# Attention stage: the values of two groups in one visit, and the first-pass products put elsewhere in the written-out order

## The chip, the cores and the metric

The kernel runs on one core of a Trainium2 chip. The metric is the device time of one execution in microseconds. A core has TensorE (PE: matrix products; its weight loads are listed apart as PEld), VectorE (DVE), ScalarE (ACT), GpSimd (POOL) and SyncE (SP, which here issues transfers). Each engine works through its own instructions in order, and the engines wait for each other through semaphores. TensorE writes its products to PSUM, which has eight banks; VectorE and ScalarE read them from there.

## The reference, cut to what matters

Two transformer layers follow each other. The change touches only the attention of the first one: two sequences of 2048 rows, 256 channels, 16 heads of 16 channels, a causal mask.

```python
Q = relu(x @ Wq + bq); K = relu(x @ Wk + bk); V = relu(x @ Wv + bv)   # (2, 2048, 256), 16 heads
scores = einsum('bqhd,bkhd->bhqk', Qh, Kh) / sqrt(16)
scores = where(key_mask == 0, NEG, scores); scores = where(tril == 0, NEG, scores)
attn = softmax(scores, axis=-1) * query_mask
out = einsum('bhqk,bkhd->bqhd', attn, Vh)        # then out + x, a normalisation, gamma and beta
```

What comes before it (normalisation, projections, a first pair of expert products) and after it (a second attention with landmarks, an expert layer) is the same in both kernels.

## The kernel before

The function `attention` works in 8 rounds of 4 heads (`n` from 0 to 7; a round is 4 of the 16 heads of one of the two sequences). The softmax needs the largest score of each query row before the exponentials can be taken, so the scores are computed twice, in two layouts.

**First pass** (`first`, 80 steps in a round, 640 in all). One step multiplies one tile of 128 queries with up to 512 keys for two heads at once, each head on 64 rows of TensorE (L993, two products side by side, into one of two slots of `c_pf`). VectorE then takes the largest score of each row: of a full stretch for both heads in one `TENSOR_REDUCE` (L1159, 48 in a round), and of the stretch with the diagonal, 128 to 512 keys wide, head by head with the mask added (L1155, 32 steps in a round). A slot is free again when VectorE is through with it (`free_slot`: a wait on `c_max_ok` for the last but one user). After the last step of a block of 512 queries six small VectorE steps (`max`) make the row maxima ready in three bf16 parts, TensorE turns them (`rows`, L999, also a user of a slot), VectorE copies them (L1182), and SP writes them with four transfers as three further rows of `c_qa`, so that the score product subtracts them itself.

**Second pass** (`score`, 36 groups of 4 steps in a round, one step per head). A group is a tile of 128 keys against a block of 512 queries, on the diagonal two smaller pieces; its steps use the full 128 rows and columns (L1012, on the diagonal also L1016 for the mask) and go into one of three slots of `c_pst`. ScalarE takes the exponential of each (L1051) into `c_prob`, which holds three groups. **Values** (`values`, one step per group): the four heads side by side, each on 32 columns of TensorE, in float32, which takes two passes (8 products, L1028), summed up in the one bank `c_po`. After the last group of a block of queries VectorE copies the bank out (`take`, L1187), TensorE turns it (`turn`, L1037, also a user of a slot of `c_pf`) and VectorE divides by the sums (L1195 to L1202).

**The order** of all these steps is one list, `steps`, made by `plan()`; every engine walks the same list and takes out its own. In the kernel before, `plan()` adds first-pass steps ahead of each score step for as long as their share of the whole lies less than `lead` ahead of the scores' share; `first_steps` does that, and puts two of the pending `max` steps behind each. The values of group j - 2 follow the fourth score of group j (`LAG`). So TensorE goes `score, first, score, score, first, score, values` in most groups. First-pass steps run about half a round ahead of the scores that need them, and the last 75 scores have none beside them; there VectorE works on the sum with the residual (`ahead`, L1066 to L1102), one piece at a time.

## Time and profile before

| | us |
|---|---|
| median of 3 runs | 2183.31 (2177.08 to 2183.34) |
| profiled execution, first to last instruction | 2184.2 |
| attention, first product to last turn | 297.0 to 1252 |
| TensorE busy over the span | 1842.2 (84%) |
| VectorE busy over the span | 1511.6 (69%) |
| ScalarE busy over the span | 1045.4 (48%) |

The profile is one execution. Times in its rows are microseconds from the start of the span; a row of a timeline has the start, the duration, the engine, the line, the operation with what it writes and reads, the count, and in brackets how long the engine had been idle before it and what ended that. Products are pipelined: a product of 512 columns shows 0.39 us, but the next one starts after less. So TensorE's pace is read from the distance between two starts, not from durations, and its busy time says little about how much room it has. The same goes to a smaller degree for VectorE, whose next instruction starts just ahead of the end of the one before.

### The profile page before, as it was taken

To read this page: it belongs to the slowest core of one execution; us is meant where nothing else is said; L and a number is where in the kernel's file an instruction comes from. 1 tells how busy PE (TensorE), PEld (TensorE's weight loads), DVE (VectorE), ACT (ScalarE), POOL (GpSimd) and SP (SyncE) were. 2 spreads that over 40 slices of the span, in tenths; PEclk is the share of its full clock that TensorE was granted. 3 is DMA by queue.
4 is the path that set the end of the run, shared out by engine and by line. 5 is a ranking of instruction groups with operands and counts; after the bars stand their busy time and mean duration, and the time that the engine had idled before them with its cause. 6 is when DMAs were issued, how large, how long until landed. Compare 5 with 4: busy or idle time off the path is not lost. (4 is left out here: it accounts for less than half of the span.)

```text
span 2184.2 us, 36363 instructions
## 1 busy us (share of the span) xinstructions
PE 1842.2 (84%) x13023; PEld 968.6 (44%) x13023; DVE 1511.6 (69%) x3492; ACT 1045.4 (48%) x1949; POOL 536.0 (25%) x592
## 2 busy tenths in 40 slices
PE   0998926899999999999899869799339788999998
PEld 0565602222222222222223246565239565888865
DVE  7986656888888888888788854387115797344456
ACT  3554403466666676666666735365003354323210
POOL 1443350000000000000330000100740786566620
PEclk9999958999999999999999979899559799999999
DMA  3466563013030304040620163000410622566656
GB/s 97 140 219 213 188 155 66 1 31 120 18 133 12 139 3 148 2 149 2 226 79 11 47 241 126 1 1 3 170 70 4 216 93 95 173 186 188 186 200 221
DMA packets 158721, 238.82 MB, mean 109 GB/s; under 512 B 19762, under 2 KB 127282, under 8 KB 156882
## 3 DMA queue, kind: packets, MB, share of 16 engines
q1 hardware_dynamic: 122706, 152.46, 23.0%
q0 software_dynamic: 23136, 75.65, 9.4%
q10 hardware_dynamic: 12704, 8.39, 1.2%
q8 instruction: 108, 1.77, 0.3%
q14 instruction: 67, 0.55, 0.1%
HBM read 116.23 MB, written 119.82 MB: 108 GB/s over the span
## 5 line engine op out<-in xcount | busy, mean ns | idle before, releaser
L1051 ACT ACTIVATE c_prob<-c_pst 128x512 f32<-128x512 f32 (+1 forms) x1152 | 602.9, 573 | 359.5 <-PE c_pst L1012 218.3
L1159 DVE TENSOR_REDUCE c_mx<-c_pf 128x2 f32<-128x1024 f32 x384 | 462.9, 1222 | 90.3 <-PE c_pf L993 87.4
L1012 PE MATMUL c_pst<-c_qa,c_ka 128*128 128x512 bf16 (+3 forms) x1280 | 394.0, 358 | 37.2 <-DMA c_qa<-c_mT 33.6
L993 PE MATMUL c_pf<-c_ka,c_qa 64*128 64x512 bf16 (+3 forms) x1280 | 234.5, 363 | 77.1 <-DVE c_mx L1159 26.4
L1028 PE MATMUL c_po<-c_prob,c_vh 128*32 128x512 f32 (+3 forms) x2560 | 297.2, 547 | 1.5 <-DVE c_osb L1187 0.5
L1155 DVE CUSTOM_DVE_ANT_0 c_spare<-c_pf,c_cut 128x384 f32<-128x384 f32 (+3 forms) x512 | 231.1, 491 | 51.9 <-PE c_pf L993 47.3
L1012 PEld LDWEIGHTS c_pst<-c_qa,c_ka 128*128 128x128 bf16 x1280 | 108.7, 97 | 283.1 <-ACT c_prob L1051 122.2
L993 PEld LDWEIGHTS c_pf<-c_ka,c_qa 64*128 64x128 bf16 x1280 | 61.9, 93 | 310.9 <-issue 126.4
L925 POOL IOTA c_zero<- 128x24 int32 x6 | 1.3, 215 | 696.8 <-PE c_po L1028 696.8
L1980 POOL DMA_INDIRECT s_parts<-x_yr,x_tags x144 | 141.0, 979 | 84.9 <-DVE x_yr L2604 61.6
L2488 PE MATMUL x_ps<-x_gu,x_xs 128*128 x576 | 136.8, 380 | 0.0
L1980 POOL DMA_INDIRECT s_slots<-x_rows,place x128 | 125.7, 982 | 37.5 <-issue 30.7
L2589 DVE TENSOR_TENSOR x_h<-x_ps,x_sg 128x256 f32<-128x256 f32 x72 | 30.6, 424 | 141.5 <-ACT x_sg L2558 134.0
L2488 PEld LDWEIGHTS x_ps<-x_gu,x_xs 128*128 128x128 f32 x576 | 104.4, 191 | 11.3
L1016 PE MATMUL c_pst<-c_negk,c_idb 128*128 128x128 bf16 x512 | 95.9, 221 | 0.0
L1028 PEld LDWEIGHTS c_po<-c_prob,c_vh 128*32 128x32 f32 x2560 | 54.6, 109 | 86.4 <-issue 42.3
L2145 DVE SCALAR_TENSOR_TENSOR i_X<-i_pm,i_eyes 128x256 f32<-128x256 f32 x48 | 20.1, 424 | 101.0 <-PE i_pm L2078 97.1
L2551 ACT COPY x_xs<-x_ps 128x512 f32<-128x512 f32 x72 | 42.2, 586 | 84.4 <-issue 65.9
L2509 PE MATMUL x_ps<-x_d,x_hT 128*128 x288 | 74.1, 380 | 0.0
L365 POOL TENSOR_TENSOR b_parts<-b_r,b_parts 128x512 bf16<-128x512 f32 x32 | 56.9, 1796 | 57.8 <-ACT b_parts L502 57.8
L1411 PE MATMUL e_pq<-e_xs,e_w 128*128 128x512 f32 x128 | 61.1, 629 | 9.5 <-ACT QT L1353 9.5
L2558 ACT ACTIVATE x_sg<-x_ps 128x256 f32<-128x256 f32 x72 | 27.7, 384 | 82.8 <-PE x_ps L2488 74.8
(378 smaller groups left out, 3007.1 us busy)
## 6 DMA issues: line engine op xcount, KB each, us to landing
s_slots<-c_zero POOLq DMA_DIRECT2D x6, 3264.0 KB, 20.4
x_xr<-s_slots SPq DMA_DIRECT2D x72, 272.0 KB
x_rows<-s_parts SPq DMA_DIRECT2D x8, 2048.0 KB, 8.7
c_qa<-s_qs SPq DMA_DIRECT2D x64, 192.0 KB, 9.0
c_ka<-s_ks SPq DMA_DIRECT2D x64, 192.0 KB, 9.8
s_qs<-b_parts SPq DMA_DIRECT2D x32, 256.0 KB, 2.4
s_ks<-b_parts SPq DMA_DIRECT2D x32, 256.0 KB, 2.7
s_vs<-b_va SPq DMA_DIRECT2D x32, 256.0 KB, 3.7
```

Of the source, the lines that this page charges most:

```text
L365: nc.gpsimd.tensor_tensor(parts[:, i, 2, :], r[:, i, :], parts[:, i, 1, :], ALU.subtract).then_inc(parts_ok, 1)
L993: mm = nc.tensor.matmul(pf[:, slot, h - fh, 0:kn], qa[r, s, h, qt * P:(qt + 1) * P], ka[r, s, h, k0:k0 + kn], start=True, stop=True, tile_ ...
L1012: mm = nc.tensor.matmul(pst[:, u % NS, at:at + qn], ka[:, s, hh, kt * P:(kt + 1) * P], qa[:, s, hh, qb * QB + q0:qb * QB + q0 + qn], start ...
L1016: mm = nc.tensor.matmul(pst[:, u % NS, at:at + P], idb[:], negk[:], start=False, stop=True)
L1028: mm = nc.tensor.matmul(po[HV * h:HV * h + HV, q0:q0 + qn], vh[:, s, kt, h, :], prob[:, a % NP, h, at:at + qn], start=(kt == 0), stop=(a i ...
L1051: nc.scalar.activation(prob[:, g % NP, hh, 0:w], pst[:, u % NS, 0:w], ACT.Exp).then_inc(exp_ok, 1)
L1155: ins = nc.vector.tensor_tensor_reduce(spare[:, h, 0:kn], pf[:, slot, h, 0:kn], cut[:, W1 - kn:], 1.0, 0.0, ALU.add, ALU.max, mx[:, fh + h ...
L1159: nc.vector.tensor_reduce(mx[:, fh:fh + 2, qt, part], pf[:, slot, :, 0:kn], AX.X, ALU.max).then_inc(max_ok, 1)
L1411: mm = nc.tensor.matmul(pq[:, i % 2, :], w[:, k, i * P:(i + 1) * P], xs[:, s, k, :], start=(k == 0), stop=(k == K - 1))
L1980: return nc.gpsimd.indirect_dma_start(out=dst, out_offset=bass.IndirectOffsetOnAxis(ap=index.bitcast(U32), axis=0), in_=src, in_offset=None)
L2488: mm = nc.tensor.matmul(pgu[:, m % 2, i, :], xs[:, m % 2, i, k, :], gu[:, k, bass.ds(e, 1), :].rearrange("p o n -> p (o n)"), start=(k == ...
L2509: mm = nc.tensor.matmul(pyr[:, m % 2, i, :], hT[:, m % 2, i, :], d[:, bass.ds(e, 1), :].rearrange("p o n -> p (o n)"), start=True, stop=True)
```

## The change

Everything lies in `plan()`; no engine's code and no buffer is touched.

- Within a block of 512 queries the groups are taken two by two. The values of both are multiplied in one visit, behind the scores of the group after them; since a block has 3, 7, 11 or 15 groups, its last one has a visit of its own. A round has 16 visits of two groups and 4 of one, in the place of 36.
- First-pass steps are put in at fewer points: ahead of a visit, behind it, and between two visits of pairs behind the third and the sixth of the eight scores (where a visit of one group follows, behind the second of its four).
- `lead` starts at 0.3 in the place of 0.21 and is capped at 0.56 in the place of 0.52. Ahead of the first score the first-pass steps are given out in 15 portions, with the `rows` step of the first block among them.
- A turn comes two groups behind the last group of its block in the place of three groups behind.

```diff
-    LAG, NP = 2, 3
+    NP = 3
     assert NG % NP == 0
+    visits = []
+    for qb in range(NB):
+        of = [g for g in range(NG) if groups[g][0] == qb]
+        visits += [of[i:i + 2] for i in range(0, len(of), 2)]
+    visit_of = {n * NG + v[-1]: [n * NG + g for g in v] for n in range(NQ) for v in visits}
+    breaks = {}
+    for n in range(NQ):
+        for v in visits:
+            for g in v:
+                breaks[n * NG + g + 1] = (3, 6) if len(v) == 2 else (2,)
+    breaks[0] = (2,)
...
     def lead(s):
-        return min(0.52, 0.21 + 0.6 * s)
+        return min(0.56, 0.3 + 0.6 * s)
...
-        for j in range(NQ * NG + LAG + 1):
+        def point(now, due=None):
+
+            first_steps(passed + lead(passed) if due is None else due)
+            if waiting and (len(steps) >= waiting[0][0] + 6 or now >= NQ * NG):
+                _, m, qb = waiting.pop(0)
+                steps.append(("rows", m, qb, 0))
+
+        for i in range(1, 16):
+            point(0, lead(0) * i / 15)
+        since = 0
+        for j in range(NQ * NG + 2):
             n, g = divmod(j, NG)
             for hh in range(HQ):
                 if n < NQ:
-                    first_steps(passed + lead(passed))
-                if waiting and (len(steps) >= waiting[0][0] + 6 or n == NQ):
-                    _, m, qb = waiting.pop(0)
-                    steps.append(("rows", m, qb, 0))
-                if done == NQ * N1:
-                    chain_step()
-                if n < NQ:
+                    if done == NQ * N1:
+                        chain_step()
                     steps.append(("score", n, g, hh))
                     passed += width[g] / sum(width) / HQ
-            if LAG <= j < NQ * NG + LAG:
-                vn, vg = divmod(j - LAG, NG)
-                steps.append(("values", vn, vg, 0))
...
+                since += 1
+                if since in breaks.get(j, ()):
+                    point(j)
+            if j - 1 in visit_of:
+                point(j)
+                for i in visit_of[j - 1]:
+                    vn, vg = divmod(i, NG)
+                    steps.append(("values", vn, vg, 0))
+                    if vg in last:
+                        steps.append(("take", vn, last.index(vg), 0))
+                point(j)
+                since = 0
+            if j >= 2 and (j - 2) % NG in last:
+                tn, tg = divmod(j - 2, NG)
+                steps.append(("turn", tn, last.index(tg), 0))
```

TensorE in the middle of the fourth round (`n` = 3), from the scores of group 13 to the values of groups 12 and 13, before. `c_pst` is written by scores, `c_pf` by first-pass steps and `c_po` by values:

```order
L1028 MATMUL c_po<-c_prob,c_vh 32x512 x4
L1012 MATMUL c_pst<-c_qa,c_ka 128x512
L993 MATMUL c_pf<-c_ka,c_qa 128x512 x2
L1012 MATMUL c_pst<-c_qa,c_ka 128x512 x2
L993 MATMUL c_pf<-c_ka,c_qa 128x512 x2
L1012 MATMUL c_pst<-c_qa,c_ka 128x512
L1028 MATMUL c_po<-c_prob,c_vh 32x512 x4
L1012 MATMUL c_pst<-c_qa,c_ka 128x512
L993 MATMUL c_pf<-c_ka,c_qa 128x512 x2
L1012 MATMUL c_pst<-c_qa,c_ka 128x512 x2
L993 MATMUL c_pf<-c_ka,c_qa 128x512 x2
L1012 MATMUL c_pst<-c_qa,c_ka 128x512
```

The same engine and place in the changed kernel:

```order
L1050 MATMUL c_po<-c_prob,c_vh 32x512 x8
L1034 MATMUL c_pst<-c_qa,c_ka 128x512 x3
L1015 MATMUL c_pf<-c_ka,c_qa 128x512 x4
L1034 MATMUL c_pst<-c_qa,c_ka 128x512 x3
L1015 MATMUL c_pf<-c_ka,c_qa 128x512 x2
L1034 MATMUL c_pst<-c_qa,c_ka 128x512 x2
L1015 MATMUL c_pf<-c_ka,c_qa 128x512 x2
L1050 MATMUL c_po<-c_prob,c_vh 32x512 x8
```

Between two first-pass steps there were at most a visit of one group and two scores; now there are a visit of two groups and three scores between the step ahead of a visit and the next one.

TensorE at the start of the stage, around the turn of the first block's maxima (`c_msp`), before:

```order
L993 MATMUL c_pf<-c_ka,c_qa 128x512 x2
L993 MATMUL c_pf<-c_ka,c_qa 128x384 x2
L993 MATMUL c_pf<-c_ka,c_qa 128x512 x2
L993 MATMUL c_pf<-c_ka,c_qa 128x384 x2
L999 MATMUL c_pf<-c_idb,c_msp 48x128
L1012 MATMUL c_pst<-c_qa,c_ka 128x512
L1016 MATMUL c_pst<-c_negk,c_idb 128x128
```

The same place in the changed kernel:

```order
L1015 MATMUL c_pf<-c_ka,c_qa 128x512 x2
L1021 MATMUL c_pf<-c_idb,c_msp 48x128
L1015 MATMUL c_pf<-c_ka,c_qa 128x384 x2
L1015 MATMUL c_pf<-c_ka,c_qa 128x512 x2
L1015 MATMUL c_pf<-c_ka,c_qa 128x384 x2
L1015 MATMUL c_pf<-c_ka,c_qa 128x512 x12
L1034 MATMUL c_pst<-c_qa,c_ka 128x512
L1038 MATMUL c_pst<-c_negk,c_idb 128x128
```

The turn has moved ahead of nine first-pass steps, behind which the score that needs it stands.

Counted in `plan()`'s two lists, from the first score on: TensorE changes between the kinds of product (64 rows, full array, 32 columns, and the narrow turn of the maxima, each a kind) 1728 times before and 1032 times after, and in one round (`n` from 1 to 6) 222 and 136 times. Between a `rows` step and the score that needs it stand in round 0 one, one, one and 9 scores before, and one, 7, 9 and 14 after.

## Rows read from the trace of the kernel before

**Rows 1.** Page, busy time (us, share, instructions) and TensorE's clock in 40 slices.

```profile
PE 1842.2 (84%) x13023; PEld 968.6 (44%) x13023; DVE 1511.6 (69%) x3492; ACT 1045.4 (48%) x1949; POOL 536.0 (25%) x592
...
PEclk9999958999999999999999979899559799999999
```

**Rows 2.** Stretch 600 to 700 us: length, PE, PEld, DVE, ACT, POOL busy; clock, DMA.

```profile
600.00:700.00 100.00, 94.50 (x639) 27.85 (x638) 85.22 (x205) 68.14 (x130) 0.30 (x1) 1.00 0.20 75
```

**Rows 3.** Timeline of POOL: start, duration, engine, operation [idle before, releaser], three round ends.

```profile
484.20 0.22 POOL L925 IOTA c_zero<- 128x24 int32 x1 [165.79 <-PE c_po L1028]
...
706.14 0.21 POOL L925 IOTA c_zero<- 128x24 int32 x1 [105.84 <-PE c_po L1028]
...
817.65 0.21 POOL L925 IOTA c_zero<- 128x24 int32 x1 [106.60 <-PE c_po L1028]
```

**Rows 4.** Timeline of TensorE in the middle of round 3: five neighbouring steps.

```profile
780.27 0.39 PE L993 MATMUL c_pf<-c_ka,c_qa 64*128 64x512 bf16 x2
...
780.59 0.39 PE L1012 MATMUL c_pst<-c_qa,c_ka 128*128 128x512 bf16 x1
...
780.91 1.06 PE L1028 MATMUL c_po<-c_prob,c_vh 128*32 128x512 f32 x8
...
781.91 0.39 PE L1012 MATMUL c_pst<-c_qa,c_ka 128*128 128x512 bf16 x1
...
782.23 0.39 PE L993 MATMUL c_pf<-c_ka,c_qa 64*128 64x512 bf16 x2
```

**Rows 5.** Timeline of both engines: a reduction's start, its pace, a slot set free.

```profile
703.55 0.39 PE L993 MATMUL c_pf<-c_ka,c_qa 64*128 64x512 bf16 x2
...
703.98 1.23 DVE L1159 TENSOR_REDUCE c_mx<-c_pf 128x2 f32<-128x1024 f32 x1 [0.66 <-PE c_pf L993]
...
710.11 1.22 DVE L1159 TENSOR_REDUCE c_mx<-c_pf 128x2 f32<-128x1024 f32 x1
...
711.24 0.17 DVE L1173 TENSOR_TENSOR c_nr<-c_nm,c_msp 128x16 f32<-128x16 f32 x1
...
711.53 1.22 DVE L1159 TENSOR_REDUCE c_mx<-c_pf 128x2 f32<-128x1024 f32 x1
...
712.80 0.10 PEld L993 LDWEIGHTS c_pf<-c_ka,c_qa 64*128 64x128 bf16 x2 [0.63 <-DVE c_mx L1159]
```

**Rows 6.** Groups by form, 380 to 1240 us: count, busy us, mean ns, idle before.

```profile
L1159 DVE TENSOR_REDUCE c_mx<-c_pf 128x2 f32<-128x1024 f32 x357 | 430.0, 1222 | 83.4 <-PE c_pf L993 80.7
...
L1155 DVE CUSTOM_DVE_ANT_0 c_spare<-c_pf,c_cut 128x512 f32<-128x512 f32 x116 | 75.3, 687 | 13.8 <-PE c_pf L993 12.8
...
L1155 DVE CUSTOM_DVE_ANT_0 c_spare<-c_pf,c_cut 128x384 f32<-128x384 f32 x116 | 59.8, 553 | 6.5 <-PE c_pf L993 4.8
...
L1155 DVE CUSTOM_DVE_ANT_0 c_spare<-c_pf,c_cut 128x256 f32<-128x256 f32 x116 | 44.3, 420 | 8.0 <-PE c_pf L993 7.5
...
L1155 DVE CUSTOM_DVE_ANT_0 c_spare<-c_pf,c_cut 128x128 f32<-128x128 f32 x114 | 28.3, 286 | 1.9 <-PE c_pf L993 1.4
```

**Rows 7.** Timeline of TensorE at the start: scores that waited for transfers.

```profile
324.45 0.59 PE L1012 MATMUL c_pst<-c_qa,c_ka 128*128 128x512 bf16 x1 [5.12 <-DMA c_qa<-c_mT]
...
348.33 0.61 PE L1012 MATMUL c_pst<-c_qa,c_ka 128*128 128x512 bf16 x1 [11.69 <-DMA c_qa<-c_mT]
...
385.46 0.61 PE L1012 MATMUL c_pst<-c_qa,c_ka 128*128 128x512 bf16 x1 [5.29 <-DMA c_qa<-c_mT]
```

**Rows 8.** Timeline of TensorE and ScalarE in the tail: one group and the next.

```profile
1225.27 0.82 PE L1012 MATMUL c_pst<-c_qa,c_ka 128*128 128x512 bf16 x3
...
1225.70 2.07 ACT L1051 ACTIVATE c_prob<-c_pst 128x512 f32<-128x512 f32 x4 [0.33 <-PE c_pst L1012]
...
1226.35 0.39 PE L1012 MATMUL c_pst<-c_qa,c_ka 128*128 128x512 bf16 x1 [0.26 <-ACT c_prob L1051]
...
1226.67 1.07 PE L1028 MATMUL c_po<-c_prob,c_vh 128*32 128x512 f32 x8
...
1227.67 0.82 PE L1012 MATMUL c_pst<-c_qa,c_ka 128*128 128x512 bf16 x3
```

More of the change, by code:

```diff
@@ L749, in plan @@
                 if n < NQ:
-                    first_steps(passed + lead(passed))
-                if waiting and (len(steps) >= waiting[0][0] + 6 or n == NQ):
-                    _, m, qb = waiting.pop(0)
-                    steps.append(("rows", m, qb, 0))
-                if done == NQ * N1:
-                    chain_step()
-                if n < NQ:
+                    if done == NQ * N1:
+                        chain_step()
                     steps.append(("score", n, g, hh))
                     passed += width[g] / sum(width) / HQ
-            if LAG <= j < NQ * NG + LAG:
-                vn, vg = divmod(j - LAG, NG)
-                steps.append(("values", vn, vg, 0))
-                if vg in last:
-                    steps.append(("take", vn, last.index(vg), 0))
-            if j >= LAG + 1:
-                tn, tg = divmod(j - LAG - 1, NG)
-                if tg in last:
-                    steps.append(("turn", tn, last.index(tg), 0))
+                since += 1
[13 more added lines that the diff above has]
+                steps.append(("turn", tn, last.index(tg), 0))
         assert done == NQ * N1 and not waiting and not chain_
```

## The prediction

> **What bounds the kernel now.** Only the attention stage is changed, from 297 to 1252 us of a span of 2184.2 us; the rest stays. Read first the busy shares and the clock by slices [rows 1]: TensorE is busy for 84% of the span, and its clock is low only where the stage starts. Then the engines' shares in a stretch in the middle of the stage [rows 2]: in 100 us PE 94.5, DVE 85.2, ACT 68.1, clock 1.00. PE's figure contains the overlap of pipelined products, so it doesn't say how near it is to its limit; DVE's 85 is near enough to be the next bound. Then the length of a round: a POOL instruction starts when the last values of a round are done, and the first of them lies at 484.20, the third at 706.14 and the fourth at 817.65 [rows 3]. Three rounds take 333.45 us, 111.1 each; rounds 1 to 6 are alike.
>
> **TensorE's work in such a round.** From the starts [rows 4]: first-pass step to score 0.32 us, score to values 0.32, values of one group to a score 1.00, score to first-pass step 0.32. Three scores behind each other start 0.215 to 0.225 apart (three take 0.82, one 0.39) [rows 8]. So a change between kinds of product costs 0.32 - 0.22 = 0.10, going in and coming out alike, and the values of one group alone are 0.90. Summed for a round: 144 scores, some of them with a mask product, about 34; 36 values 31; 80 first-pass steps 15; four turns of 0.5, 2; 222 changes of kind 21. That is 103 of the 111 us: TensorE sets the pace and waits for some 8 us.
>
> **VectorE's work in the same round** [rows 5, 6]. The next instruction starts 1.13 us behind the start of a 1.22 us reduction (710.11, 711.24). The masked steps are two instructions each; less an overlap of 0.08 for each, like the reductions', they take 1.21, 0.95, 0.68 and 0.41 us for 512, 384, 256 and 128 keys. So the first pass is 48 x 1.13 + 8 x 3.25 = 80 us. The small steps of the maxima, the copies and the divisions are the rest of the busy time, which is 0.852 x 111.1 = 94.7 in all, counted to the end of each instruction; less 0.09 for each of some thirty behind which nothing is queued, I take 92 us. VectorE has 19 us of room in a round, in bits.
>
> **What the change removes.** 86 changes of kind in a round, 8.6 us of TensorE; the kind of a second group's values follows its like, so a visit of two groups is 1.00 + 0.90 = 1.90. No step from first-pass to values stands in the trace; I take the 0.10 of the others, since all that were seen cost the same, and the bounds 0 and 0.2 would move a round by at most 2 us. If TensorE alone decided, that would be the end of it.
>
> **What it adds: a gap for VectorE at each visit of two groups.** VectorE gets its work through two slots. Let a first-pass step start on TensorE at t, just ahead of a visit. The visit starts at t + 0.32 and lasts 1.90, three scores and the step into the next first-pass product take 0.22 + 0.22 + 0.32, and VectorE starts on that product 0.43 after it (703.55 to 703.98) [rows 5]: t + 3.40 in round figures. What has VectorE by then? The two slots at most. If the step at t had to wait for its slot (the next product starts 0.05 behind the end of the reduction: 711.53 + 1.22, 712.80 [rows 5]), VectorE is 0.15 into the other one and is done with both at t + 2.26 - 0.15 = t + 2.11. So it stands idle for at least 1.29 us, more where one of the two is a narrow masked step. Before, the same way was first-pass step, score, visit, score, first-pass step: 0.32 + 0.32 + 1.00 + 0.32 + 0.43 = 2.39, of which two full slots cover nearly all. Sixteen such gaps are 21 us in a round; VectorE has 19 to give. A visit of one group has no gap: there is one group and two scores, and the copy of 0.68 fills what is left.
>
> The points behind a visit don't help: the due share moves only with scores, and none stand between the point ahead of a visit and the one behind it. In the whole list no first-pass step stands directly behind a visit (before, 117 did).
>
> From this the **length from visit to visit** can be worked out. If VectorE decides, it is 3.40 + 0.15 + VectorE's time for all its slots' users between the two visits but the last two (which it works on during the gap). ScalarE sets a lower end: three slots of `c_pst`, so the eighth score waits for the end of the fifth exponential; by the tail's rows (first exponential 0.43 behind its score, four in 2.07, so one each 0.49, the fourth score 1.08 behind the first [rows 8]) the eighth starts 3.04 behind the first, and with 0.32, 0.32 and 1.90 the length is at least 5.5. Two examples. Groups 12 and 13: reduction, masked 512, reduction, reduction: 3.55 + 1.13 + 1.21 = 5.9 (before, the same content took TensorE 5.7 and its waits). Groups 21 and 22: reduction, masked 384, a turn (about 1.0 of VectorE, an estimate for its four small instructions), reduction, masked 384, reduction: 3.55 + 4.24 = 7.8. The sixteen of a round come to 5.5 to 7.9, 106 in sum (less 0.1 where the step ahead of the visit is narrow); the four visits of one group with their copies to 2.8 to 3.5, 12 in sum. Together **118 us for a round against 111.1**, 6.8 more. It agrees with the other way of counting: 92 of work and 16 gaps of 1.6 on average.
>
> **The start.** The scores of the first blocks wait for the transfers of their maxima, 5.1, 11.7 and 5.3 us, the second behind the load of the next round's operands [rows 7]. Now nine first-pass steps stand between the first turn and its score, and 7 and 9 scores with four or more first-pass steps before the next two: the first and third wait go, the second shrinks to some 4 us. But VectorE is the bound of round 0, which holds 101 first-pass steps in 36 groups, and it gets sixteen gaps here too. From the first score to the end of the round, 324.45 to 484.20 [rows 3, 7], are 160 us, and VectorE's work in them is some 120 by the durations above (about a quarter more than in a later round, as the pairs run ahead). Its 40 idle us, with the waits in them, become 26 of gaps, 4 of the second wait and 3 of work for steps that now come earlier. With what stays between them I take -5 us (bounds -15 and +3).
>
> **The tail.** Behind the last first-pass step only scores, exponentials and values run. A group takes 2.40 us there (1225.27 to 1227.67) with ScalarE's slots in the way: the fourth score waits 0.26 us [rows 8]. Two groups in one go take 3.04 + 0.32 + 1.90 = 5.26 in the place of 4.80. Ten visits of two groups: +4 us.
>
> **The sum.** Rounds 1 to 6: 6 x 6.8 = +41. The part of round 7 with first-pass steps, 33 of 80: +3. Start -5, tail +4. 2184.2 + 43 = 2227; the median lies 0.9 under the profiled span, and the estimates of the start lean down by a little: **2225 us**.
>
> On this mechanism the Trainium skill has a sentence that speaks against the change, in "TensorEngine Tiling (Array Packing)", section "Performance Considerations": tiling speeds up the products, not what empties PSUM behind them. The rows here agree, with 85 us of VectorE in 100.
>
> **Rivals.**
> - **The changes of kind decide (faster).** If VectorE's idle bits before can be moved about so that a gap costs nothing (a longer queue than I think, or first-pass work that isn't late when it comes late, since it runs half a round ahead), TensorE's sum holds: 111.1 - 8.6 a round, 6.4 rounds -55, start -5, tail +4: 2128 us. For it: TensorE's 103 of 111. Against: its products for VectorE stand in order in the same queue as the visits, so a late VectorE stops the visit itself. The condition is that fewer than 3 of the 4 or 5 first-pass steps between visits find their slot taken. The skill's page on tiling says in "Key Properties" that changing the tiling mode drains TensorE; the trace agrees with 0.10 us a change, and by that rule alone the time would be this rival's.
> - **Gaps at their least (about the same).** If both slots are full with 1.13 each at each visit, and light and heavy stretches even out: 92 + 16 x 1.29 is 113, +1.6 a round, +10; start -12, tail +4: 2186 to 2192. Against it: seven of the sixteen steps ahead of a visit are masked ones of 128 to 384 keys, and lengths under 5.5 aren't possible.
> - **The clock.** In the start the clock fell to 0.5 in a slice with long waits [rows 1]. If TensorE's longer waits brought it down in the rounds, a part of 95 us of work per round would take twice as long; a tenth at half speed is +9 a round, 2260 or more. Against: waits of a microsecond occur now, at clock 1.00 [rows 2].
>
> **Chances.** Forecast 60% (2205 to 2245), changes of kind 16%, least gaps 17%, clock 7%. About 0.3%, 6.5 us, is what a measurement of this kernel can tell from no change. Faster by more: 0.16 and a bit of the third, 0.18; within: 0.10; slower: 0.72. For 8 in 10 the range goes from 2180, under the least gaps, to 2248.
>
> **What would show it.** In the changed profile: distances of the POOL instruction behind each round of 116 to 119 us (right), about 113 (least gaps) or 103 (changes of kind). VectorE idle for 1.2 to 2 us behind each visit of two groups, ended by a first-pass product. First-pass products on TensorE waiting for VectorE much more than now. Visits of two groups 1.90 long, then the next kind. A wait before the second block's scores in round 0 of some 4 us and none at the first and third. In the tail 5.26 us for two groups. Wrong it would be if VectorE's share in the middle rose over 90 in 100 us: it should fall to about 80.

## The result, and the profile after

| | before | after |
|---|---|---|
| median | 2180.22 us (2177.08 to 2183.34, 4 runs) | 2241.47 us (2239.39 to 2242.66, 4 runs) |
| profiled execution, span | 2184.2 | 2238.7 |
| mean granted clock | 0.939 | 0.937 |

The changed kernel is slower: ratio 1.0269, interval 1.0251 to 1.0286. Forecast were 2225 us, range 2180 to 2248. In the changed kernel the lines of `attention` lie 22 further down (L1015 for L993, L1050 for L1028, L1181 for L1159).

First the page: engines over the whole span, and TensorE's clock in 40 slices.

```profile
PE 1830.6 (82%) x13023; PEld 980.7 (44%) x13023; DVE 1509.0 (67%) x3492; ACT 1010.5 (45%) x1949; POOL 536.0 (24%) x592
...
PEclk9999958999999999999999989999759899999999
```

TensorE is busy for less of a longer span. The middle of the stage says it more sharply. Windows of the changed kernel: from:to, length, then PE, PEld, DVE, ACT and POOL busy, granted clock, DMA share, GB/s.

```profile
600.00:700.00 100.00, 84.51 (x570) 26.59 (x570) 76.45 (x193) 56.48 (x114) 0.56 (x1) 0.97 0.22 78
1100.00:1200.00 100.00, 83.45 (x532) 24.34 (x530) 75.19 (x176) 55.65 (x111) 32.12 (x29) 0.93 0.32 107
```

Against [rows 2] PE fell from 94.5 to 84.5, DVE from 85.2 to 76.5 and ACT from 68.1 to 56.5. All three lost, so nothing got busier: they wait for each other. The clock of 0.97 is new as well; [rows 2] has 1.00.

Then the rounds. The POOL instruction behind rounds 0, 2, 3 and 5, as in [rows 3] (start, length, what it is, idle before it):

```profile
477.93 0.22 POOL L947 IOTA c_zero<- 128x24 int32 x1 [160.94 <-PE c_po L1050]
...
719.06 0.21 POOL L947 IOTA c_zero<- 128x24 int32 x1 [115.73 <-PE c_po L1050]
839.25 0.21 POOL L947 IOTA c_zero<- 128x24 int32 x1 [114.14 <-PE c_po L1050]
...
1081.19 0.21 POOL L947 IOTA c_zero<- 128x24 int32 x1 [115.75 <-PE c_po L1050]
```

Five rounds in 603.26 us, 120.65 each, against 111.1. The whole difference of the spans, by stretches:

| stretch | before | after | difference | forecast |
|---|---|---|---|---|
| up to the end of round 0 | 484.2 | 477.9 | -6.3 | -5 |
| rounds 1 to 5 | 555.6 | 603.3 | +47.7 | +34 |
| round 6 | 117.6 | 126.9 | +9.3 | +7 |
| round 7 with the tail | 94.8 | 101.1 | +6.3 | +7 |
| behind the stage | 932.0 | 929.5 | -2.5 | 0 |
| sum | 2184.2 | 2238.7 | +54.5 | +43 |

Round 6 took 117.6 us already before, and not 111.1 like rounds 1 to 5: the prediction had called rounds 1 to 6 alike.

**The clock, round by round.** Windows of the changed kernel from round 1 to round 6, and of the kernel before for rounds 1 to 5 in one and round 6; the figure behind the POOL group is the granted clock.

```profile
477.93:597.26 119.33, 102.54 (x725) 33.27 (x724) 92.93 (x225) 71.09 (x144) 2.46 (x3) 0.99 0.20 69
597.26:719.06 121.80, 104.30 (x726) 33.76 (x725) 93.80 (x225) 71.20 (x144) 2.23 (x3) 0.97 0.20 68
...
959.38:1081.19 121.81, 104.33 (x726) 33.83 (x725) 93.78 (x225) 71.10 (x144) 2.23 (x4) 0.97 0.20 68
1081.19:1208.10 126.91, 107.02 (x726) 33.88 (x725) 96.17 (x225) 71.20 (x144) 38.74 (x39) 0.95 0.40 131
```

```profile
484.20:1039.79 555.59, 524.73 (x3623) 160.27 (x3621) 471.16 (x1121) 376.71 (x720) 11.37 (x16) 1.00 0.22 74
1039.79:1157.40 117.61, 106.89 (x727) 32.26 (x726) 94.97 (x225) 75.45 (x144) 38.77 (x39) 0.97 0.43 142
```

One minus the granted clock, times the length, is what TensorE lost where it was working. Added up over windows of 4 or 5 us that is 11.9 us in rounds 1 to 5 (before, 0) and 6.8 in round 6 (before, 3.4). So each of rounds 1 to 5 lost 2.4 us to the clock on average and is 118.3 long without that. Behind the stage it is the other way round: the same sum is 87.2 us before and 80.1 after, over a stretch whose work is the same. Over the whole span it is 134.3 and 142.5.

**Where a round's time is.** Each matrix product's start can be set against the next one's. Products of one kind have a pitch of their own, a step to another kind costs 0.10 more, and what is beyond that is a wait, or the low clock. Per round, over rounds 1 to 5:

| us of TensorE in a round | own pitch | changes of kind | waits | low clock | round |
|---|---|---|---|---|---|
| before | 83 | 21.1 | 7.5 | 0 | 111.1 |
| after | 83 | 12.9 | 22.4 | 2.4 | 120.65 |

The gain is there as counted, 8.2 us. The waits grew by 14.9. They stand before first-pass products (8.8 between two of them, 5.0 behind a score), before turns (3.2) and before row products (3.0), all of which need a slot that VectorE frees, and before scores, which need ScalarE (2.8). The parts are good to some tenths, since they hang on the pitch taken for each kind.

**A gap, row by row.** TensorE, then VectorE, in round 3 of the changed kernel (start, length, engine, line, count; in brackets the idle time and what ended it):

```profile
756.96 0.39 PE L1015 MATMUL c_pf<-c_ka,c_qa 64*128 64x512 bf16 x2
757.28 1.92 PE L1050 MATMUL c_po<-c_prob,c_vh 128*32 128x512 f32 x16
759.13 0.82 PE L1034 MATMUL c_pst<-c_qa,c_ka 128*128 128x512 bf16 x3
759.89 0.61 PE L1015 MATMUL c_pf<-c_ka,c_qa 64*128 64x512 bf16 x4
...
762.82 0.39 PE L1015 MATMUL c_pf<-c_ka,c_qa 64*128 64x512 bf16 x2 [0.26 <-DVE c_mx L1177]
```

```profile
756.82 2.35 DVE L1181 TENSOR_REDUCE c_mx<-c_pf 128x2 f32<-128x1024 f32 x2
760.32 1.23 DVE L1181 TENSOR_REDUCE c_mx<-c_pf 128x2 f32<-128x1024 f32 x1 [1.15 <-PE c_pf L1015]
```

The step ahead of the visit starts at 756.96, and 0.32 later the sixteen values products of two groups. VectorE has the two slots' reductions (2.35 from 756.82) and nothing more. Its next product starts at 759.89 and it starts on that at 760.32: 3.36 behind the step, where the prediction had 3.40. Idle for 1.15. When both slots are full again, TensorE waits in its turn (0.26 at 762.82).

Over rounds 1 to 5 VectorE's time between the end of one first-pass reduction and the start of the next came to 25.8 us in a round behind the sixteen visits of two groups, 1.61 each (0.15 of it the low clock, seven visits of eighty); of other kinds, another 10.4. Small steps of VectorE that stand in between (of the maxima, copies, divisions) are counted as idle in this measure. Before, it was 26.1 in all. Taken away from the rounds' length, this measure leaves 85 us before and 84.5 after: VectorE's own work didn't change, the idle time, the low clock in it, is the round's whole difference. The groups of the two engines for the stage (busy us, mean ns | idle before, by releaser), against [rows 6]:

```profile
L1181 DVE TENSOR_REDUCE c_mx<-c_pf 128x2 f32<-128x1024 f32 x342 | 408.1, 1220 | 117.8 <-PE c_pf L1015 117.5
...
L1015 PE MATMUL c_pf<-c_ka,c_qa 64*128 64x512 bf16 x794 | 145.6, 386 | 47.4 <-DVE c_mx L1181 32.4 <-DVE c_mx L1177 7.9 <-DVE c_att L1224 4.5
```

Idle before full reductions rose from 83.4 to 117.8 (357 and 342 of them in the same window of 860 us), and TensorE's product waits for VectorE in the same stretch. Each of two engines is idle for want of the other, which a share of busy time alone doesn't tell.

### The profile page after: what moved, and what is told of

It is laid out like the page before. It is cut to its first block and busy times, and to the rows that moved or that the text cites. A ratio compares the mean times of both kernels' runs of the same rounds, so it can differ in the third digit from the quotient of the medians.

```text
span 2238.7 us, 36363 instructions
## 1 busy us (share of the span) xinstructions
PE 1830.6 (82%) x13023; PEld 980.7 (44%) x13023; DVE 1509.0 (67%) x3492; ACT 1010.5 (45%) x1949; POOL 536.0 (24%) x592
## 5 line engine op out<-in xcount | busy, mean ns | idle before, releaser
L1073 ACT ACTIVATE c_prob<-c_pst 128x512 f32<-128x512 f32 (+1 forms) x1152 | 568.8, 583 | 452.1 <-PE c_pst L1034 296.3
L1181 DVE TENSOR_REDUCE c_mx<-c_pf 128x2 f32<-128x1024 f32 x384 | 458.8, 1221 | 130.6 <-PE c_pf L1015 130.1
L1034 PE MATMUL c_pst<-c_qa,c_ka 128*128 128x512 bf16 (+3 forms) x1280 | 366.6, 357 | 13.1 <-ACT c_prob L1073 2.1
L1015 PE MATMUL c_pf<-c_ka,c_qa 64*128 64x512 bf16 (+3 forms) x1280 | 217.9, 363 | 135.3 <-DVE c_mx L1181 64.5
L1050 PE MATMUL c_po<-c_prob,c_vh 128*32 128x512 f32 (+3 forms) x2560 | 287.5, 571 | 0.0
L1015 PEld LDWEIGHTS c_pf<-c_ka,c_qa 64*128 64x128 bf16 x1280 | 55.7, 93 | 305.9 <-DVE c_mx L1181 124.3
L1050 PEld LDWEIGHTS c_po<-c_prob,c_vh 128*32 128x32 f32 x2560 | 70.4, 114 | 131.9 <-issue 96.5
L2326 ACT ACTIVATE k_e<-k_d 128x1024 f32<-128x1024 f32 x32 | 33.9, 1060 | 76.3 <-POOL k_en L2262 52.8
```

The source lines that it names most:

```text
L1015: mm = nc.tensor.matmul(pf[:, slot, h - fh, 0:kn], qa[r, s, h, qt * P:(qt + 1) * P], ka[r, s, h, k0:k0 + kn], start=True, stop=True, tile_ ...
L1034: mm = nc.tensor.matmul(pst[:, u % NS, at:at + qn], ka[:, s, hh, kt * P:(kt + 1) * P], qa[:, s, hh, qb * QB + q0:qb * QB + q0 + qn], start ...
L1050: mm = nc.tensor.matmul(po[HV * h:HV * h + HV, q0:q0 + qn], vh[:, s, kt, h, :], prob[:, a % NP, h, at:at + qn], start=(kt == 0), stop=(a i ...
L1073: nc.scalar.activation(prob[:, g % NP, hh, 0:w], pst[:, u % NS, 0:w], ACT.Exp).then_inc(exp_ok, 1)
L1181: nc.vector.tensor_reduce(mx[:, fh:fh + 2, qt, part], pf[:, slot, :, 0:kn], AX.X, ALU.max).then_inc(max_ok, 1)
```

## The experiments

A figure for a round is the mean of rounds 1 to 5, from the POOL instruction's starts. "Kinds" is the number of changes of kind in a round (before 222, after 136). "Lost to the clock" is the sum of one minus the granted clock over short windows, as above, in the one profiled execution. Ratios are against the kernel before.

### Visits of two groups alone, in the order of before

```diff
-            if LAG <= j < NQ * NG + LAG:
-                vn, vg = divmod(j - LAG, NG)
+            for i in visit_of.get(j - 1, ()):
+                vn, vg = divmod(i, NG)
                 steps.append(("values", vn, vg, 0))
...
-            if j >= LAG + 1:
-                tn, tg = divmod(j - LAG - 1, NG)
-                if tg in last:
-                    steps.append(("turn", tn, last.index(tg), 0))
+            if j >= 2 and (j - 2) % NG in last:
+                tn, tg = divmod(j - 2, NG)
+                steps.append(("turn", tn, last.index(tg), 0))
```

> The order of before (first-pass steps spread between the scores, the old lead), with the values of two groups in one visit and nothing else. TensorE's changes of kind in a round fall from 222 to 195. If the gap for VectorE decides (theory): first-pass step, score, visit of 1.9 us, score, first-pass step are 0.32 + 0.32 + 1.9 + 0.32 + 0.43 = 3.3 us, two slots cover 2.1, so 1.2 us are lost in most of the 16 visits; a round takes 116 to 119 us in the place of 111, the kernel some 2215 to 2235. If the changes of kind decide: 27 x 0.1 = 2.7 us a round less, about 2163.

Measured: 2208.92 us (2207.07 to 2216.32), ratio 1.0142 (1.0109 to 1.0174); a round 115.1 (0.7 of it lost to the clock), kinds 195. The visits of two by themselves cost 4 us in a round. VectorE's gap behind them is 1.24 on average and not 1.61, since the order of before may put a first-pass step ahead of every score. Round and time lie just under what was expected.

### The changed kernel with more first-pass steps behind each visit

```diff
-                point(j)
+                if n < NQ:
+                    point(j, passed + lead(passed) + 1.1 / N1)
+                else:
+                    point(j)
```

> The changed kernel with visits of two groups, but behind each visit one first-pass step more may be taken (the due share there is raised by 1.1 steps), which then is missing behind the third score. The number of changes of kind stays (1038 against 1032). If the gap for VectorE decides (theory): from the step ahead of a visit to the start of the next reduction it is now 0.32 + 1.9 + 0.43 = 2.65 in the place of 3.40 us, so 0.75 x 16 = 12 us a round come back; 108 to 111 us a round, the kernel about 2165 to 2185. If something else made the changed kernel slower (the clock alone, transfers, ScalarE's slots, which this lengthens by nothing and shortens by nothing), it stays near 2241.

Measured: 2221.47 us (2217.02 to 2225.88), ratio 1.0183 (1.0156 to 1.0211); a round 118.3, 1.7 of it lost to the clock. The gap did what was expected. From the step ahead of a visit (698.31) to the next reduction (700.92) it is 2.61 us in the trace of this kernel, where 2.65 was expected:

```profile
698.31 0.39 PE L1018 MATMUL c_pf<-c_ka,c_qa 64*128 64x512 bf16 x2 [0.28 <-DVE c_mx L1180]
...
698.63 1.92 PE L1053 MATMUL c_po<-c_prob,c_vh 128*32 128x512 f32 x16
...
700.49 0.39 PE L1018 MATMUL c_pf<-c_ka,c_qa 64*128 64x512 bf16 x2
...
700.92 0.69 DVE L1180 CUSTOM_DVE_ANT_0 c_spare<-c_pf,c_cut 128x512 f32<-128x512 f32 x1 [0.40 <-PE c_pf L1018]
```

But a little later:

```profile
704.02 0.39 PE L1018 MATMUL c_pf<-c_ka,c_qa 64*128 64x512 bf16 x2
...
704.34 1.93 PE L1053 MATMUL c_po<-c_prob,c_vh 128*32 128x512 f32 x24
...
703.68 2.36 DVE L1184 TENSOR_REDUCE c_mx<-c_pf 128x2 f32<-128x1024 f32 x2 [1.45 <-PE c_pf L1018]
```

A reduction waited 1.45 us at 703.68, but that isn't a visit's gap: the visit comes at 704.34, and before its product (703.25) stood six scores with no first-pass step between them. In the same count as above the idle time behind the visits of two fell from 25.8 to 13.3 us in a round, and that between first-pass steps with no visit between them rose from 7.6 to 17.5. The steps put at the visit's second side were taken from between the scores, since their number is given. So the cause (VectorE unfed over a long stretch of TensorE's) is borne out, and the cure moved the stretch elsewhere. The expected 108 to 111 us a round didn't come: my expectation left out where the steps would come from.

### The changed kernel with visits of one group

```diff
-        visits += [of[i:i + 2] for i in range(0, len(of), 2)]
+        visits += [[g] for g in of]
```

> The changed kernel, its points and its longer lead, but with the values of one group in each visit (36 visits a round; a first-pass point behind the second score and ahead of the visit). Changes of kind in a round: 182 (before 222, changed 136). By the gap: first-pass step, visit of 1.0, two scores, first-pass step are 0.32 + 1.0 + 0.22 + 0.32 + 0.43 = 2.3 us, nearly covered by two slots (2.1), so no gap is left and TensorE's 40 changes less show: 107 us a round, about 2155. If the points or the lead are what hurts in the changed kernel and not the visits of two, it stays over 2200.

Measured: 2161.99 us (2158.58 to 2165.18), ratio 0.9917 (0.9888 to 0.9945); a round 110.1 with nothing lost to the clock, kinds 182. The visits are all that differs from the changed kernel, and they make 79 us. The change's points and its longer lead, without the visits of two, are faster than before. Of the 24 us of the span most are won in the start: the instruction behind round 0 comes at 462.56 instead of 484.20. The rounds after it win only a microsecond each, although 40 changes of kind are gone; expected were 107 a round.

### Visits of one group, first-pass steps behind every third score and behind the visit

```diff
-        visits += [of[i:i + 2] for i in range(0, len(of), 2)]
+        visits += [[g] for g in of]
...
-                breaks[n * NG + g + 1] = (3, 6) if len(v) == 2 else (2,)
+                breaks[n * NG + g + 1] = (3,)
...
             if j - 1 in visit_of:
-                point(j)
```

> A version meant to be better than both: visits of one group, one first-pass point behind the third score and one directly behind each visit, none ahead of it (three scores, first-pass step, score, values, first-pass step). Changes of kind in a round: 170. The way between two first-pass steps is 0.32 + 0.32 + 1.0 = 1.6 or three scores, about 1.0, so VectorE is never without work for long, and ScalarE's fourth score has waited by the time the first-pass step is done. Theory: TensorE's sum of 103 less 52 x 0.1 is 98, with waits of 4 to 6 a round of 102 to 105 us, the kernel about 2125 to 2150. If VectorE's two slots bind here too, 110 and more.

Measured: 2151.28 us (2148.29 to 2152.42), ratio 0.9865 (0.9839 to 0.9892); a round 108.8 with nothing lost to the clock, kinds 170. Faster than both kernels. Of the expected 102 to 105 the last 4 us didn't come: its waits are 10 of the 108.8. Its window, in the columns of before:

```profile
600.00:700.00 100.00, 90.82 (x654) 29.23 (x661) 87.21 (x212) 66.17 (x132) 2.22 (x3) 1.00 0.17 58
```

DVE 87 in 100, more than before and eleven more than after.

### VectorE's reductions cut short, in the order of before and in the changed order

Here each first-pass reduction of a full stretch (48 of the 80 steps of a round) reads 128 of its 512 keys, so the row maxima are those of a part of the keys only; all else stays. One kernel has the order of before, the other the changed one.

```diff
-                        nc.vector.tensor_reduce(mx[:, fh:fh + 2, qt, part], pf[:, slot, :, 0:kn], AX.X, ALU.max)
+                        nc.vector.tensor_reduce(mx[:, fh:fh + 2, qt, part], pf[:, slot, :, 0:P], AX.X, ALU.max)
```

> The kernel before, in which VectorE's reductions of full stretches (48 of 80 first-pass steps in a round) read 128 keys per head in the place of 512: the row maxima are taken from a part of the keys only. Nothing else changes, so this shows what TensorE and ScalarE alone would take. VectorE's 92 us a round fall to some 55. TensorE's sum is 103, so a round takes 104 to 106 us in the place of 111; the kernel about 2140.

> The same cut (reductions of full stretches read 128 of 512 keys per head) in the changed kernel. If the changed kernel is slow because VectorE is without work behind a visit of two groups and can't make it up (theory), then with little work for VectorE the gap costs nothing and only ScalarE's three slots are left (5.5 us per visit of two, 100 a round): 98 to 102 us a round, faster than its counterpart by 3 to 6 us a round, about 2105 to 2120. If visits of two are slow by themselves (the clock, dearer changes of kind), it is slower than its counterpart again, over 2150.

Measured: order of before 2156.32 us (2155.14 to 2157.34), ratio 0.988, a round 110.0; changed order 2122.43 us (2114.96 to 2127.57), ratio 0.973, a round 105.7. Windows of the one and of the other:

```profile
600.00:700.00 100.00, 95.20 (x654) 28.91 (x654) 55.21 (x211) 68.90 (x132) 2.22 (x3) 1.00 0.15 47
```

```profile
600.00:700.00 100.00, 94.39 (x700) 31.71 (x696) 53.84 (x206) 66.87 (x137) 2.22 (x3) 1.00 0.25 83
```

VectorE's share is 54 to 55 in both, and TensorE is at the 94 to 95 of [rows 2] in both. Now the changed order wins, by 4.3 us in a round (3.3 without the 1.0 that the order of before lost to the clock), where with the full reductions it loses 9.5 (7.1 without the clock). TensorE's waits, the low clock set apart, are 5.1 in the order of before (from 7.5) and 9.9 in the changed one (from 22.4). So 12.5 us of the changed kernel's waits hang on VectorE's time, and what stays is some 4 before scores, for ScalarE, and 6 of others. This decides the case: the gain of the rarer changes of kind is real, and it is VectorE's work that turns it into a loss. Both rounds are longer than expected, since waits of 5 to 10 us stay even so.

### First-pass steps by VectorE's time, visits of one group

The kernel with steps behind every third score, with half a group's share of first-pass steps due at each of its two points:

```diff
-    cost1 = [f[3] + 64 for f in first]
+    cost1 = [(2 * (0.07 + f[3] / 960) if f[2] + f[3] == (f[1] + 1) * P else 1.13) for f in first]
...
+            half = passed + width[g] / sum(width) / 2
...
-                if since in breaks.get(j, ()):
-                    point(j)
+                if since == 3 and n < NQ:
+                    point(j, half + lead(passed))
```

> The version with visits of one group (three scores, first-pass step, score, values, first-pass step), now with the first-pass steps given out by VectorE's time for them (1.13 us for a full stretch, 0.42 to 1.21 for masked ones) and half a group's share due at each of the two points. In the version before it 13 of 36 visits had no step behind them and others two in one place. Changes of kind in a round: 182 in the place of 170 (+1 us for TensorE). If VectorE's idle bits are what is left to win (theory), a round takes 103 to 106 us in the place of 108.8, the kernel about 2115 to 2135; if the number of changes of kind decides, 110 a round and 2158.

Measured: 2150.63 us (2149.63 to 2152.25), ratio 0.9856 (0.9837 to 0.9876); a round 109.2 (0.3 lost to the clock), kinds 182, waits 8.7. No different from the kernel that counts keys, and not the expected 103 to 106 a round. VectorE's idle time per visit fell to 0.40, below the 0.44 there, and twelve more changes of kind took that back. Weighing the steps by VectorE's time gave nothing here.

### The changed kernel with the lead capped as before

```diff
-        return min(0.56, 0.3 + 0.6 * s)
+        return min(0.52, 0.3 + 0.6 * s)
```

> The changed kernel with the cap of the lead of before (0.52 in the place of 0.56), the start left as it is. The steps and the visits are the same, only shifted against each other by some three first-pass steps. Theory: no change beyond 0.3% (2235 to 2248). If the longer lead itself costs something, under 2230.

Measured: 2223.27 us (2221.63 to 2228.34), ratio 1.0196 (1.0173 to 1.022); a round 119.4. A miss: no change was expected, and 18 us came. In the traces 5 of them lie in round 0 (it ends at 472.80), 6 in rounds 1 to 5 and 7 in round 6. Without the clock rounds 1 to 5 are 116.7 each against 118.3, and the waits before row products are 1.4 us in a round where they were 3.0: as much. Row products carry VectorE's maxima, and the cap changes how many first-pass steps stand around them; that this is the reason wasn't tested. In round 6 half of the 7 is the clock, 3.4 lost against 6.8. For round 0 the trace gives no single place.

### Visits of two groups, fed in four shares

The changed kernel's visits; from visit to visit the first-pass steps are given out by VectorE's time in four shares: ahead of the visit, behind it, behind the third and behind the sixth score.

```diff
-    cost1 = [f[3] + 64 for f in first]
+    cost1 = [(2 * (0.07 + f[3] / 960) if f[2] + f[3] == (f[1] + 1) * P else 1.13) for f in first]
...
+            if j == 0 or j - 2 in visit_of:
+                end = min([i for i in visit_of if i >= j - 1] or [NQ * NG - 1]) + 1
+                begin, share = passed, sum(width[i % NG] for i in range(j, end + 1)) / sum(width)
+                pts = {3: 0.25, 6: 0.5} if end > j else {2: 0.4}
...
-                if since in breaks.get(j, ()):
-                    point(j)
+                if since in pts and n < NQ:
+                    point(j, begin + pts[since] * share + lead(begin))
...
-                point(j)
+                point(j, begin + (0.75 if end >= j and len(visit_of[j - 1]) > 1 else 0.7) * share + lead(begin))
```

> The changed kernel's visits of two groups, with its first-pass steps given out by VectorE's time in four equal shares between two visits: ahead of the visit, behind it, behind the third and the sixth score (around visits of one group: ahead, behind, and behind the second score). It differs from the earlier run with a step on both sides in that no stretch of six scores is left without a step. Changes of kind in a round: 150 (changed 136, before 222). If what costs is only that VectorE is without work (theory), 16 gaps of 0.6 us are left, TensorE's sum is 97 and its waits about 10: 106 to 109 us a round in the place of 120.7, the kernel about 2125 to 2150, as good as visits of one group. If visits of two cost by something else too, it stays over 115 a round and over 2200.

Measured: 2185.99 us (2178.77 to 2190.01), ratio 1.0007 (0.9993 to 1.0021); a round 113.7 (0.3 lost to the clock), kinds 150: between the two outcomes that were expected. TensorE, and the reduction behind the visit:

```profile
707.88 1.92 PE L1054 MATMUL c_po<-c_prob,c_vh 128*32 128x512 f32 x16
...
709.74 0.50 PE L1019 MATMUL c_pf<-c_ka,c_qa 64*128 64x512 bf16 x4
```

```profile
710.17 1.23 DVE L1185 TENSOR_REDUCE c_mx<-c_pf 128x2 f32<-128x1024 f32 x1 [0.40 <-PE c_pf L1019]
```

A step directly behind the visit, and the reduction waits 0.40 instead of 1.15. The order of the steps, with the visits of two kept, thus gives back 55 of the 61 us; some 17 of them are the clock (lost in rounds 1 to 6 of the profiled executions: 1.7 against 18.8). Idle behind the visits is 10.6 us in a round, but stretches without a visit hold 15.3, and TensorE's waits are 16.4 of a round. Behind a visit of two VectorE is still without work for 0.66 us on average, with a first-pass step on either side of it; behind one of one group it is 0.44 in the order with steps behind every third score.

### The two orders with visits of one group, lead capped

The edit is that of the cap above, on the kernel with steps behind every third score and on the one by VectorE's time.

> The version with visits of one group, a first-pass point behind the third score and one behind the visit, with the cap of the lead at 0.52 in the place of 0.56. In the changed kernel this cap alone gave 18 us, 6 in rounds 1 to 5, 5 in round 0 and 7 in round 6. If that was a matter of which steps fall beside the long visits, little of it comes here: within 5 us of 2151. If the longer lead costs by itself (transfers of a round arriving late for it in rounds 0 and 6), 2135 to 2142.

> The same cap in the version with the shares by VectorE's time. Changes of kind 178 in the place of 182. Same question as the run beside it: near 2150 if the cap matters only beside visits of two, 2135 to 2142 if a longer lead costs by itself.

Measured: 2157.11 us (2155.6 to 2160.52), ratio 0.9875, a round 110.0; and 2167.39 us (2159.33 to 2171.02), ratio 0.992, a round 112.1. With the clock set apart the orders differ little: lost to it are 1.0 and 2.7 us in a round, and the rest is 109.0 and 109.4, where the orders without the cap have 108.8 and 108.9. A longer lead costs nothing by itself, then: neither came down to 2135 to 2142. Of the 17 us of the second, some 10 to 12 are the clock (0.937 to 0.940 in its six executions, 0.940 to 0.945 without the cap). The 6 us of the first are open. Its profiled execution (2160.52, clock 0.937) lost 12 us more to the clock than that without the cap, but its other three had 0.942 to 0.944, as there, and still took 2155.6 to 2158.0 against 2148.3 to 2152.4. The best orders stay those without the cap, 1.4% under the kernel before.

The kernel before with only the longer lead, and the changed one with the old start of the lead, weren't tried, so the lead's own share in the start isn't shown.

## Why the prediction was right, and where it wasn't

**Side and mechanism held.** The forecast said that visits of two groups leave VectorE with nothing once both slots are reduced, sixteen times in a round, 1.6 us on average; measured 1.61, 0.15 of it the low clock and with VectorE's small steps counted in, so that the second digit is luck. It said t + 3.40 from the step ahead of a visit to the next reduction; 3.36 in the rows above. It said that VectorE's share falls to about 80; 76.5. With VectorE cut short the changed order wins, as a mechanism of VectorE's slots demands. The rival by which the changes of kind decide had 2128 us; only the kernel with VectorE's work cut (2122) behaves like that.

**No price for the step from first-pass to values** stood in the trace of before. It was taken as the 0.10 of the others: 756.96 to 757.28 is 0.32, so it holds. A visit of two is 1.85 (757.28 to 759.13), taken as 1.90.

**The round is where time is missing:** 120.65 against 118, of which 2.4 is the clock. The order itself gives 118.3, so the sum held; two of its terms did not. Ten of the sixteen lengths from visit to visit, read in round 3, 719.06 to 839.25. The prediction gives two of them, and 5.5 to 7.9 for all:

| groups | 12, 13 | 14, 15 | 16, 17 | 18, 19 | 21, 22 | 25, 26 | 27, 28 | 29, 30 | 31, 32 | 33, 34 |
|---|---|---|---|---|---|---|---|---|---|---|
| forecast | 5.9 | | | | 7.8 | | | | | |
| measured | 5.86 | 7.18 | 7.40 | 7.17 | 6.49 | 7.66 | 6.64 | 5.48 | 6.75 | 5.38 |

The visits of two come to 103.9 in all, where the forecast had 106. "The four visits of one group with their copies to 2.8 to 3.5, 12 in sum" measured 3.58, 5.14, 3.81 and 3.75; the 5.14 bears a visit at half clock (3.47 in the rounds where it ran at full), so it is 14.6. "A visit of one group has no gap" is true of its own gap. But a length bears the gap of the visit that it starts with, and all four stand behind a visit of two. The pair behind a single visit is shorter in return: 21 and 22 had 7.8 and took 6.49. I had put each gap one visit too early, +2.6 and -2.1, and that the two errors all but cancel is luck.

**The step that failed is the clock.** The sum had nothing for it. It stood as a rival of 7% that would cost 9 us a round (some 2280 us then, where the prediction wrote "2260 or more"), one thing or the other, with "waits of a microsecond occur now, at clock 1.00" against it. It came as a part: 11.9 us of the 47.7 in rounds 1 to 5 and 3.4 of the 9.3 in round 6, 15 us, more than the 11.5 by which the forecast's sum of the spans fell short. Without the clock the rounds 1 to 6 took 35.8 + 5.9 = 41.7 us more than before; the forecast was 41. The reading that the clock is low only where the stage starts was too quick: [rows 1] has 5 in two slices behind the stage, and round 6 of the kernel before stood at 0.97.

**Start:** -6.3 against -5. But the prediction's own three terms, 26, 4 and 3 in the place of 40, would be -7, and it isn't as told: a transfer's wait ahead of scores is left at 0.7 us, one wait of one, where 4 were expected for the second block. (Counted in the lists, 0, 6, 8 and 13 scores stand between a `rows` step and the score that needs it, not 1, 7, 9 and 14, and 9, 4, 6 and 8 first-pass steps; before, 0, 0, 0 and 8 scores: the needed score itself had been counted.) Waits of TensorE in the stage (us, times, longest):

```profile
PE c_pf L1015 <- DVE c_mx L1181: 64.5, 107, 1.5
PE c_pf L1015 <- DVE c_mx L1177: 27.2, 47, 2.1
...
PE c_pst L1034 <- DMA c_qa<-c_mT: 0.7, 1, 0.7
```

The three waits of [rows 7] were 22.1 us together; round 0 got only 6.3 of them. With visits of one group 18 to 22 come through (round 0 ends at 462.56 to 465.84). So visits of two take 12 to 15 us of the start's gain back there, by the gaps that they leave in round 0 too. Some of it may be the clock, whose loss up to 440 us is 42.7 in the changed kernel and 37.6 in the one that differs by the visits alone.

**Tail:** 5.26 for two groups; measured 5.21, 1279.34 to 1284.55.

```profile
1279.34 1.92 PE L1050 MATMUL c_po<-c_prob,c_vh 128*32 128x512 f32 x16
1281.20 0.82 PE L1034 MATMUL c_pst<-c_qa,c_ka 128*128 128x512 bf16 x3
...
1284.55 1.92 PE L1050 MATMUL c_po<-c_prob,c_vh 128*32 128x512 f32 x16
```

**The median** lies 2.8 over the span of the profiled execution, where the prediction took 0.9 under it (four executions of the kernel before put its median, 2180.22, 4.0 under). With the 11.5 of the spans and the 1.3 that the prediction took off for the start's estimates, this is the rest of the way from 2225 to 2241.

**What stays open:** what brings the clock down, how much of the changed kernel's 32 us over the one with visits of two alone is the longer lead and how much the place of the steps, and why orders with visits of one group stay at 109 a round: their waits are 9 to 10 us, more than the 7.5 of before, though VectorE is idle for some 2.5 us less. In the one by VectorE's time 6.7 of them stand behind a first-pass step, before another one, a row product or a turn.

## What to carry to other kernels

Fusing two visits of a bound engine saves what stands between them and makes one long stretch out of two short ones: compare the stretch, with all that stands before the neighbour's next product, with the work that the neighbour's buffers hold. Here that is 3.4 us against two slots of 1.13, and 8 us saved a round cost 15 of waits and 2 of clock. When steps move to where they are wanted, look at where they come from, since a queue is then empty there. Two engines at 85 and 95 in 100 left little for any order here: what helped was the evenness of the feeding (steps every third score, one visit a group), and that with fewer changes of kind gave 1.4%.

## What the hardware showed that I had not expected

**Half clock behind short waits.** Windows of the changed kernel, 2 us each, and TensorE's rows in them:

```profile
784.00:786.00 2.00, 1.26 (x9) 0.50 (x13) 1.41 (x6) 0.29 (x2) 0.00 (x0) 0.72 0.00 0
786.00:788.00 2.00, 2.00 (x16) 0.52 (x12) 0.00 (x0) 0.00 (x0) 0.00 (x0) 0.50 0.02 3
```

```profile
784.74 0.22 PE L1021 MATMUL c_pf<-c_idb,c_msp 128*48 128x128 bf16 x1 [0.76 <-DVE c_mx L1181]
...
784.89 3.59 PE L1050 MATMUL c_po<-c_prob,c_vh 128*32 128x512 f32 x24
...
789.38 1.23 DVE L1181 TENSOR_REDUCE c_mx<-c_pf 128x2 f32<-128x1024 f32 x1 [3.98 <-PE c_pf L1015]
```

TensorE was idle for 0.69 us (up to 782.94) and again for 0.76; then the clock is at 0.50, the lower of its two levels, while it works without a break. The visit (two groups; the second is on the diagonal and comes in two pieces, so 24 products) takes 3.52 (784.89 to 788.41), where two groups take 1.85, and VectorE behind it is idle for 3.98. Such a stretch costs 1.7 us, and the rounds 1 to 5 hold seven in the changed kernel and none in the one before; in the others the low clock costs 0 to 13.7 us there. That doesn't follow the sum of TensorE's waits: visits of two in four shares have 16.4 us of waits in a round and 1.7 us lost in all five, the order by VectorE's time with the cap 9.5 and 13.7. Nor does the order alone fix it: the same place just behind the start of a round has a stretch in rounds 2, 4 and 5 of the changed kernel (603.98, 846.33, 965.79) and none in rounds 1 and 3. Between orders that differ little up to 12 us came or went in this way, each read in one execution, which is more than the orders' own effect; so the clock has to be taken out before two orders are compared.

**A change of kind costs the same whatever it is.** 0.10 between first-pass products on 64 rows, scores on the full array and values on 32 columns, in all of the pairs that occur, the one new in the changed kernel (first-pass to values: 0.32 from 756.96 to 757.28, where a product of 512 columns is otherwise followed after 0.22) included.
